# One core, a four-layer graph stack: in the first layer's loop, the raise of a visit's own tiles goes ahead of the third unit of sums

## What is computed

```python
S1 = jnp.einsum('id,kdh->ikh', Q, A1)
S2 = jnp.einsum('jd,kdh->jkh', K, A2)
kidx = jnp.clip(edges, 0, nb - 1)
e = S1[rows[:, None], kidx] + S2[rows[None, :], kidx]
valid = (edges >= 0)[..., None]
e = jnp.where(valid, jax.nn.leaky_relu(e, negative_slope=NEG_SLOPE), 0.0)
attn = jax.nn.softmax(e, axis=1)
out = jnp.einsum('ijh,jhd->ihd', attn, Vh).reshape(n, h * d)
```

## Time and profile before

| | us |
|---|---|
| median of 3 runs | 990.64 |
| lowest, highest | 990.62, 991.81 |
| the profiled execution | 995.63 |
| its span | 993.8 |
| TensorE busy | 888.3 (89% of the span) |
| VectorE busy | 717.7 (72%) |
| ScalarE busy | 542.7 (55%) |
| GpSimd busy | 536.8 (54%) |

### The profile page before, as it was taken

The page is one execution under the profiler, slowest core; times in us unless marked ns, Lnnn a source line. Parts: engine busy times, 40 slices in busy tenths (PEclk is TensorE's granted clock), DMA queues, the critical chain, the costliest instruction groups (busy, mean ns, idle before and its releaser), DMA issues.

```text
span 993.8 us, 17974 instructions
## 1 busy us (share of the span) xinstructions
PE 888.3 (89%) x6998; PEld 333.9 (34%) x6998; DVE 717.7 (72%) x1158; ACT 542.7 (55%) x941; POOL 536.8 (54%) x662
## 2 busy tenths in 40 slices
PE   6899999999999999999999289999969669999950
PEld 5733222222222222222224222233333234556630
DVE  3555557888788788888874778411669658999977
ACT  2589666666666666666663177001130248888830
POOL 3267659889898988989882100000000017778832
PEclk9979999999999999999999579999959966999995
DMA  8572111121211111021000000000000000000000
GB/s 171 134 140 41 54 58 41 37 70 24 76 37 59 42 47 61 22 78 35 20 18 12 1 1 1 1 1 1 1 1 1 1 0 1 1 1 1 1 1 21
DMA packets 23035, 32.64 MB, mean 33 GB/s; under 512 B 14587, under 2 KB 14715, under 8 KB 21926
## 3 DMA queue, kind: packets, MB, share of 16 engines
q1 hardware_dynamic: 20646, 23.11, 7.8%
q0 software_dynamic: 2304, 8.39, 4.7%
HBM read 38.58 MB, written 1.29 MB: 40 GB/s over the span
## 4 chain that ended last, share of the span: by engine, by line
PE 74%; DVE 19%; issue 4%; ACT 2%; DMA 1%; DVEq 0%; POOL 0%; ACTq 0%
PE ps L1275 23%; PE ps L1285 11%; PE ps L1423 8%; PE ps L1262 6%; DVE big L498 5%; PE ps L1254 4%; PE ps L1371 3%; PE ps L1449 3%; PE ps L1485 3%; PE ps L1131 2%; DVE big L847 2%; DVE big L495 2%; PE ps L1457 1%; PE ps L1242 1%; DVE big L632 1%
## 5 line engine op out<-in xcount | busy, mean ns | idle before, releaser
L632 DVE COPY_PREDICATED big<-mask,ps 128x512 f32<-128x512 uint8 x512 | 341.5, 729 | 113.8 <-PE ps L1262 110.1
L441 POOL TENSOR_SCALAR big<-big 128x512 f32<-128x512 f32 x512 | 355.8, 714 | 74.5 <-PE ps L1285 72.5
L998 ACT ACTIVATE ps<-ps 128x512 f32<-128x512 f32 x512 | 268.6, 583 | 141.8 <-PE ps L1254 141.5
L1275 PE MATMUL ps<-big 128*32 128x512 f32 x2048 | 253.7, 600 | 0.0
L467 POOL TENSOR_TENSOR big<-big 128x512 f32<-128x512 f32 x34 | 56.3, 1657 | 266.3 <-ACT big L1081 266.3
L1285 PE MATMUL ps<-big 128*32 128x512 f32 x1024 | 134.5, 597 | 0.0
L1254 PE MATMUL ps<-op_r,op_l 18*128 18x512 bf16 x512 | 111.7, 384 | 3.9 <-DVE big L632 2.2
L1275 PEld LDWEIGHTS ps<-big 128*32 128x32 f32 x2048 | 53.8, 109 | 119.8 <-issue 110.4
L1485 PE MATMUL ps<-big 66*128 66x512 f32 (+3 forms) x160 | 74.6, 605 | 1.3 <-DVE big L819 1.3
L1262 PE MATMUL ps<-op_r,op_l 9*128 9x512 bf16 x512 | 74.7, 388 | 0.7 <-ACT ps L998 0.5
L498 DVE TENSOR_TENSOR big<-big,mask 128x1024 f32<-128x1024 f32 (+4 forms) x72 | 66.9, 956 | 5.3 <-ACT big L1023 3.8
(11 more groups left out here) (277 smaller groups left out, 1093.3 us busy)
## 6 DMA issues: line engine op xcount, KB each, us to landing
big<-max_scratch SPq DMA_DIRECT2D x8, 1024.0 KB, 4.8
big<-rden_scratch SPq DMA_DIRECT2D x30, 256.0 KB, 3.3
big<-in_adj_dram POOLq DMA_DIRECT2D x12, 512.0 KB, 9.4
op_l<-split_scratch SPq DMA_DIRECT2D x56, 36.0 KB
op_r<-split_scratch SPq DMA_DIRECT2D x56, 36.0 KB
work<-in_adj_dram POOLq DMA_DIRECT2D x2, 512.0 KB, 13.3
h_nat<-in_adj_dram POOLq DMA_DIRECT2D x2, 512.0 KB, 11.8
x_nat<-in_x_dram SPq DMA_DIRECT2D x1, 512.0 KB, 5.1
```

The lines of the kernel that those rows point to most:

```text
L441: pool.tensor_scalar(ring[:, k % RING, :], vrow[:, head % 2, i0:i0 + HALF], HUGE, g0[:, head, jt:jt + 1], ALU.min, ALU.max).then_inc(s["ba ...
L632: dve.copy_predicated(ring[:, k % RING, :], mask[:, jt, i0:i0 + HALF], ps[:, slot("tile", k), :])\
L998: act.activation(ps[:, at_slot, :], ps[:, at_slot, :], ACT.Relu, scale=-1.0).then_inc(s["relus"], 1)
L1275: m = pe.matmul(ps[32 * w:32 * (w + 1), MAIN, :], vp[:, head, jt + w // 2, 32 * (w % 2):32 * (w % 2 + 1)], ring[:, (u + w // 2) % RING, :] ...
```

## The change

In a visit with three units the tiles that the visit has just crossed are raised ahead of its third unit. The visit after it then doesn't raise. All other visits are as before.

```diff
-            for v in range(LAST):
-                for kind, k in trio(v - 1):
+            def raises(v):
+
+                for kind, k in trio(v):
                     if kind == "tile":
                         raise_floor(k)
+
+            def long_visit(v):
+
+                return v >= 0 and units(v + 1) - units(v) == 3
+
+            for v in range(LAST):
+                if not long_visit(v - 1):
+                    raises(v - 1)
                 for kind, k in trio(v):
                     if kind == "tile":
                         cross(k)
@@
                 for u in range(units(v), units(v + 1)):
+                    if long_visit(v) and u == units(v) + 2:
+                        raises(v)
                     if u % 3 < 2:
                         aggregate(4 * (u // 3) + 2 * (u % 3))
                     else:
```

## The result

| | before | after |
|---|---|---|
| median, us | 990.91 (4 runs) | 998.25 (4 runs) |
| lowest, highest | 990.62, 991.81 | 996.70, 1000.01 |
| ratio | | 1.0073, 95% interval 1.0056 to 1.0089 |
| profiled execution, its span | 995.63, 993.8 | 996.70, 994.9 |

The change makes the kernel slower by 0.73%, 7.3 us (5.5 to 8.8). The four executions of before in the table are also among the short ones of those sets.

What follows compares the result with a forecast made beforehand. TensorE, 99% busy with 11.6 us of waits for late crosses, was taken to bound the loop. 9.0 - 2.6 - 2.9 - 0.4 + 0.7 = +3.8 us gave 994.4 us, 0.38% slower, range 989.2 to 998.5.

Steps and rivals of the forecast that it cites:

- The cost of the second switch: TensorE, 36 long visits: one more change between f32 and bf16 products costs 0.25 us each, +9.0 us.
- Rival 1: TensorE's second switch is nearly free, 0.10 us each, 3.6 us in all: 988.3 us, faster; chance 0.11.
- rival 4: TensorE's second switch costs a full group, 0.46 us each: +11.4 us, 1002 us; chance 0.04.
- What b gives back: Second visit after the long one, nine stalls: earlier raises start DVE's selects sooner, ending late crosses, -2.6 us.
- what c gives back: Third visit after the long one, eight stalls: the block addition ends before the next raises, -2.9 us.
- Rival 3: Nothing comes back: crosses in the second and third visits after the long one stall as before, 1000.3 us; chance 0.11.
- The bias: Where DVE adds the bias, one stall of about 1.2 us: the earlier raise returns 0.4 us once.
- In L, 0 us: Long visit, eight late crosses waiting on DVE: their raises don't move, so the 4.9 us of stalls stay.
- rival 2: The long visit's late crosses vanish too, returning 4.9 us: 989.5 us, no measurable change; chance 0.06.
- The relus in a, +0.7: Visit after the long one, nine times: relus end late, delaying the last raise by some 0.08 us, +0.7 us.
- The sum: All terms of the loop together give +3.8 us, and the same 3.8 us is put on the median: 994.4 us.
- The weight load: TensorE's load for the raises isn't pulled ahead of running matmuls, which speaks for the middle switch cost.

Runs made afterwards that it cites:

- s1_half: The change made in only 18 of the 36 long visits, against the kernel before; ratio 0.9994 (0.9978 to 1.0009).
- p2_place_after: The changed kernel with VectorE's reciprocals and block additions moved to its widest window; median 992.90 us, ratio 1.0001 to the kernel before.
- p1_place_before: The kernel before with VectorE's reciprocals, block additions and bias moved to its widest window, TensorE's order unchanged; median 991.27 us, ratio 0.9981.
- c1_no_add: The changed kernel with a copy of 16 columns in place of each block addition; one execution, 993.40 us.

## Why the prediction was right, and where it was off

- **What bounds the kernel** was right. TensorE's own order sets the loop, and all other time in it was late crosses.
- **The cost of the second switch**, 0.25 us a time (0.24 by its own terms, 0.92 less 0.68), was right: 0.244 from the changed kernel's trace (387.40 less 378.61, by 36), 0.247 from the pair with other orders on VectorE. It was worked out from one lone group of raises at the loop's end and one lone cross. Rival 1, a nearly free switch, and rival 4, a full second group, are both excluded.
- **What b gives back** (-2.6) and **what c gives back** (-2.9) were right to the count: no stall is left there but the bias's. Rival 3 is excluded. **The bias** gave back 0.6 instead of 0.4: 1.23 to 0.60.
- **In L, 0 us** is the term that was mis-sized: it was +1.7. The step that failed reads "DVE had no backlog that an earlier start could shorten", and stopped there. That was true, and rival 2 fell with it. But the step took the addition's 0.78 us as its own length. In the same rows the same instruction took 1.05 us at 187.13. By moving VectorE against GpSimd, the change put it where it takes 0.95 or 0.96 us six times and 1.12 or 1.13 twice, and stalls of 0.79 and 0.95 us followed. In s1_half, with the addition at 0.77 us, the stall is 0.6. That the shift against GpSimd is what lengthened it is our reading of the traces; no run takes GpSimd's instructions away.
- **The relus in a, +0.7** was wrong. The last raise is late by the foretold 0.08 us (the group at 196.32 is 0.46 us long instead of 0.39), but the first unit follows at 0.54 as ever. The likely reason is that the six products run in two waves of three, and the late one found room in the second; no run tests it. Term: 0.
- **The sum** for the loop was +3.8 where it is +4.4. It left out 1.7 us in L and had 0.7 us too much for the relus, so that its two main errors half cancelled; the bias and the switch, 0.2 us each, make up the rest. The larger error is in the step from the loop to the time, "the same 3.8 us on the median": the measured +7.3 us holds 2 to 3 us that the loop's trace doesn't.
- **The weight load.** The prediction read from one row that the raises' load isn't pulled ahead, and the row has no wait. Other rows of the same load have one, at 192.82 in the changed kernel for instance, put down to the relus. The load of the denominators behind the early raises settles it. It waits for no semaphore, and still begins with its own product at 193.15:

```profile
193.15 0.16 PEld L1285 LDWEIGHTS ps<-big 128*32 128x32 f32 x8 [0.23 <-issue]
```

## What to carry to other kernels

An engine at 99% busy can still be waiting. Read the starts of its recurring group, subtract the undisturbed length, and list what is left with its period; here that gave 26 stalls with three causes. Before earlier work is paid for with one more switch of the bound engine, ask whether the late step can be moved instead: an order on the waiting engine that puts its side work into the widest window cost nothing and returned 1.0%, where the earlier raise paid 8.8 us for 6.1 in b, c and at the bias, and lost 1.7 again in L. And take an instruction's length from all its rows, not from the one beside the stall.

## What the hardware showed that was not expected

The block addition on VectorE, two sources of 512 f32 columns in SBUF, takes 0.67 us with GpSimd idle, 0.62 to 1.2 us mostly while GpSimd is busy, 2.26 to 2.37 us three times in p2_place_after, and 4.40 us twice in p1_place_before. There it began at 283.50 and 454.33 and ended only when GpSimd's run of 13 instructions did. Issued 0.44 us earlier in the same kind of run it took 0.82 us. The copy of 16 columns in c1_no_add varies in the same way, 0.15 to 0.69 us. The Trainium skill, "SBUF — State Buffer", section "Who interferes with whom", says that a VectorE instruction with two inputs in SBUF contends with a GpSimd instruction that reads SBUF. Its section "SBUF: two separate sides" says that the one that starts first holds the shared ports for its whole instruction and the other is fully blocked. The traces agree with a block: twice the addition ended 0.55 us after GpSimd's run. But one of GpSimd's instructions takes 0.67 us there (8.69 us by 13), and 3.85 us of the 4.40 are the rest of the run. By these rows VectorE was passed over several times in succession. What decides whether it is passed over was not measured; the one thing known is that 0.44 us earlier it wasn't.
